# A decoder layer on one core: another issue order, causal bias matmuls of 128 and 64 columns, and shorter constant set-up

## The reference

```python
x = _layernorm(x + attn(x))            # q,k,v with bias; causal softmax over 1024 keys; output projection with bias
x = _layernorm(x + xattn(x, ctx))      # 64 context keys per batch, masked by the mask of batch 0
x = _layernorm(x + ffn(x))             # gate and up to 1024, silu(gate) * up, down to 256
# ffn: ternary weights from mean |w|, activations rounded to 8 bits by each row's maximum
```

## Time and profile before

| | us |
|---|---|
| median of 3 runs (lowest, highest) | 862.05 (861.85, 863.84) |
| profiled execution | 861.85 |
| its span | 860.1 |
| PE busy (share of the span) | 804.4 (94%) |
| DVE busy | 673.9 (78%) |
| ACT busy | 578.8 (67%) |
| POOL busy | 389.6 (45%) |

### The profile page before, as it was taken

One profiled execution on the slowest core, in us unless ns is written; L12 is line 12 of the kernel. 1 busy time (PEld: TensorE's weight loads), 2 busy tenths in 40 slices (PEclk: granted clock), 3 DMA queues, 4 the chain that ended last, 5 costly groups with the idle time before them and its releaser, 6 DMA issues.

```text
span 860.1 us, 21760 instructions
## 1 busy us (share of the span) xinstructions
PE 804.4 (94%) x8207; PEld 388.0 (45%) x8235; DVE 673.9 (78%) x1179; ACT 578.8 (67%) x759; POOL 389.6 (45%) x629
## 2 busy tenths in 40 slices
PE   7888999999999999999999999999999999999875
PEld 5433334344553434534464344633545443445533
DVE  5899898668977798768998589874898858836598
ACT  2377865468865698555875669666696569864486
POOL 6724465446443346542535544472534503442335
PEclk9999999999999999999999999999999999999899
DMA  7713224301223212201221111220131000010001
GB/s 227 203 48 91 49 52 106 94 2 34 48 57 94 63 38 55 72 1 30 72 64 38 38 50 46 63 69 14 39 94 32 26 2 2 2 50 2 2 2 50
DMA packets 47814, 45.50 MB, mean 53 GB/s; under 512 B 9698, under 2 KB 43874, under 8 KB 47714
## 3 DMA queue, kind: packets, MB, share of 16 engines
q1 hardware_dynamic: 43698, 39.12, 17.4%
q0 software_dynamic: 1536, 3.15, 1.6%
q10 hardware_dynamic: 2480, 1.84, 0.8%
HBM read 14.55 MB, written 4.19 MB: 22 GB/s over the span
## 4 chain that ended last, share of the span: by engine, by line
PE 73%; DVE 12%; ACT 8%; issue 3%; DMA 1%; POOL 1%; SPq 1%; ACTq 0%; POOLq 0%; DVEq 0%
PE ps L995 14%; PE ps L1010 14%; PE ps L808 10%; PE ps L970 7%; PE ps L823 5%; DVE shift L1324 5%; PE ps L942 3%; PE ps L869 3%; PE ps L954 3%; ACT probs L1113 3%; PE ps L899 2%; PE ps L911 2%; PE ps L797 2%; PE ps L894 2%; PE ps L880 2%
## 5 line engine op out<-in xcount | busy, mean ns | idle before, releaser
L1113 ACT ACTIVATE probs<-ps 128x1024 f32<-128x1024 f32 (+3 forms) x384 | 296.1, 810 | 121.2 <-PE ps L995 119.0
L1324 DVE TENSOR_REDUCE shift<-ps 128x2 f32<-128x1024 f32 (+2 forms) x224 | 248.5, 1143 | 49.5 <-PE ps L970 28.5
L995 PE MATMUL ps<-q_stack,k_stack 64*128 64x512 bf16 (+3 forms) x1536 | 174.3, 325 | 10.9 <-ACT probs L1113 3.2
L1010 PE MATMUL ps<-probs,v_aug 128*32 128x512 f32 (+3 forms) x1536 | 155.7, 495 | 0.1
L697 POOL TENSOR_SCALAR_AFFINE_SELECT probs<-probs 128x512 f32<-128x512 f32 x128 | 80.6, 638 | 154.5 <-ACT probs L1113 153.7
L970 PE MATMUL ps<-k_stack,q_stack 64*128 64x512 bf16 (+3 forms) x768 | 112.2, 326 | 10.8 <-ACT probs L1113 3.8
L995 PEld LDWEIGHTS ps<-q_stack,k_stack 64*128 64x128 bf16 x1536 | 54.8, 94 | 122.4 <-ACT probs L1113 44.9
L1324 DVE TENSOR_REDUCE shift_h<-ps 128x4 bf16<-128x512 f32 (+2 forms) x96 | 96.8, 1043 | 13.9 <-PE ps L976 13.3
L970 PEld LDWEIGHTS ps<-k_stack,q_stack 64*128 64x128 bf16 x768 | 39.8, 93 | 98.8 <-ACT probs L1113 38.6
L1010 PEld LDWEIGHTS ps<-probs,v_aug 128*32 128x32 f32 x1536 | 34.9, 108 | 42.2 <-issue 31.4
L1237 DVE TENSOR_REDUCE shift<-ps 128x8 bf16<-128x512 f32 x64 | 40.1, 683 | 14.9 <-PE ps L880 14.8
(11 more groups left out here) (188 smaller groups left out, 1344.6 us busy)
## 6 DMA issues: line engine op xcount, KB each, us to landing
q_stack<-part_sb SPq DMA_DIRECT2D x168, 64.0 KB, 2.0
k_stack<-part_sb SPq DMA_DIRECT2D x144, 64.0 KB, 2.1
xT<-in_x_cols SPq DMA_DIRECT2D x8, 512.0 KB, 4.0
xt<-in_x SPq DMA_DIRECT2D x8, 512.0 KB, 3.8
out_x<-xt SPq DMA_DIRECT2D x7, 512.0 KB, 2.8
k_stack<-part_sb POOLq DMA_DIRECT2D x48, 64.0 KB, 2.3
q_stack<-shiftT SPq DMA_DIRECT2D x128, 1.0 KB
q_stack<-part_sb ACTq DMA_DIRECT2D x24, 64.0 KB, 2.5
```

The lines of the kernel that those rows point to most:

```text
L995: mm = pe.matmul(ps[:, u.banks[i], 0:BANK - off], k_stack[rows, part, h, kb * P:(kb + 1) * P], q_stack[rows, part, c, h, off:BANK], start= ...
L1010: mm = pe.matmul(ps[DV * i:DV * (i + 1), SUM_BANK, off:BANK], v_aug[:, kb, at:at + DV], probs_of(b, n)[:, i, :], start=first, stop=last)
L1113: act.activation(probs_of(b, n)[:, 2 * p:2 * p + 2, :], pair(u)[:, :, 0:BANK - off], ACT.Exp).then_inc(probs_ready, 1)
L1324: dve.tensor_reduce(to[:, :, pairs[0]:pairs[-1] + 1, qb % TH], pair(u)[:, :, 0:len(pairs) * w].rearrange("p j (h w) -> p j h w", w=w), AX. ...
```

## The change

Four things change. First, the whole string `ORDER` is another one; the number of units of each kind is the same. Second, the causal bias of a group is added by two matmuls of 128 columns (the rows of the first 64 queries) and two of 64 columns (the first 64 keys for the other queries), where it was four of 64 columns; the number of matmuls and of weight loads is the same. Third, `pick_h` has 192 columns for 256, and POOL builds it and `causal` with 4 selections for 12; a `drain` on POOL behind `make_masks` is gone. Fourth, `stir` runs 15 transposes for 25.

```diff
 ORDER = (
-    "ffwr6sfffr0sgr6sr1r0r6sr2m01m45m23r6ggm45m01m23m45r6ffffm01m23gr4m01m56m23a01a45am01a23w6a45m01fffaa23a45am2"
+    "r6sr5sr6sr5r6sgr5m01gm23m45r6m01ggm45m01r6fm23m01m23wfm01m45r3fm01a45w6r3m01a45fffam23m01a45w6a23afm45fa01oa"
...
-        pick_h, causal = sb("pick_h", [P, 2 * P], BF16), sb("causal", [P, P], BF16)
+        pick_h, causal = sb("pick_h", [P, P + HALF], BF16), sb("causal", [P, P], BF16)
...
             for rows in four:
-                made(pool.affine_select(out=pick_h[rows], in_=pick_h[rows], compare_op=ALU.not_equal, fill=1.0, base=0,
-                                        pattern=[[-1, 2 * P]], channel_multiplier=1))
...
+                made(pool.affine_select(out=pick_h[rows], in_=pick_h[rows], compare_op=ALU.not_equal, fill=1.0, base=HALF,
+                                        pattern=[[-1, P + HALF]], channel_multiplier=1))
                 made(pool.affine_select(out=causal[rows], in_=causal[rows], compare_op=ALU.is_ge, fill=NEG, base=0,
-                                        pattern=[[0, 2], [-1, HALF]], channel_multiplier=1))
...
+                                        pattern=[[-1, P]], channel_multiplier=1))
...
                         make_masks()
-                        pool.drain()
...
-                        stir(u, 25)
+                        stir(u, 15)
...
                     if diag:
-                        for part in range(2):
-                            at, keys = slice(part * P, (part + 1) * P), slice(part * HALF, (part + 1) * HALF)
-                            for s, rows in enumerate(four):
-                                mm = pe.matmul(ps[:, u.banks[s], end - P + part * HALF:end - HALF + part * HALF], pick_h[rows, at],
-                                               causal[rows, keys], start=False, stop=part == 1)
+                        for s, rows in enumerate(four):
+                            pe.matmul(ps[:, u.banks[s], end - P:end], pick_h[rows, HALF:P + HALF], causal[rows, :],
+                                      start=False, stop=False)
+                        for s, rows in enumerate(four):
+                            mm = pe.matmul(ps[:, u.banks[s], end - HALF:end], pick_h[rows, 0:P], causal[rows, 0:HALF],
+                                           start=False, stop=True)
```

More of the change, by code:

```diff
@@ L77 @@
[L77 to L79 removed]
+    "r6sr5sr6sr5r6sgr5m01gm23m45r6m01ggm45m01r6fm23m01m23wfm01m45r3fm01a45w6r3m01a45fffam23m01a45w6a23afm45fa01oa"
+    "23afm01a45m23a45aa01m45m23w6cm01wfa45om23saa45ooa01m23or6m45m01axa23fwfm45a23saa01a23m45r6ao23om45wom01a23m4"
+    "5oa01m23a45xow6a01m23a45m01oga23m45o01om23wa45a01oa23a45m01oaa23m01a45gm23m01am45oom23a01oa45m01aa23m45soa01"
@@ new lines @@
+    "am45r6m01ooa23m45a01o23m45sa01om23a45m01a23a45m01oa23m01a45ga23m01a45m23oam01wa45oa23aa01oa45rm23am01a45a23a"
+    "m45a23m01a45gam23om01m45m23r6m01oom23oa45m01ra23o45am01a23a45oaa23m45a01m23goom01awa45oa23aa01m45r6rm01m23a4"
+    "5aa01om45m23a01o01oaa23m45a01em23eaa01m45oa23m01ooogm45a23o01m45a23p01om23m45bm01p6p5a01a23a45opm01m23r6m01p"
+    "a45a23om45rp01m23m45p6m01m23p5pp6p1p0a23bgaop6gm45a01pr3p6p5a01p2p6aa34a01op6m01p24arm01r6m01ra23p45p02p45r6"
+    "p45a01p23m01aa45op23p01a45om23p01om45a23m01p6m23oa01m45p6o01a23a45oa01goa23pm45rm01r6a23m45a01ppaoa23pa45pap"
@@ new lines @@
+    "rom01m23r6a01a45oaa01m23a45p01m45aom23p6m01m45p3p2om01oop6m45gp3o01p2p6p5p3p2a01gpa34m56apr2xppgp1p0a34a56op"
+    "m12aa34a56pppar0p45a23p6p1oa45apa23a01m45ppr6pam01p23p5p6a23a01m45ooop6aa23a01po45aoa23oopa01ppm23p45p6m01p2"
+    "3p6p3papp01otoa45a23m01p6xo45m01ea23p6a23pa01a45oa23om01a45a23pa01m45oam23p45m01a23m45p6m01m23p5pp6p1p0a23op"
+    "6aa23pm45ba01am23a01p6p1p0a23oap6a23m45a01op6oom01p24om01r6m01p23p04rp23r6a23p01p45m01a23p45rp01o23om45p01om"
+    "23a01m45p6m01m23a45p6a01a23gopa45pa01am23m45a23m01m45a23apoa01a23aa45poa01pm23paa45m01r6m23oom01p45m23a01m45"
@@ new lines @@
+    "p6m23op1gm45ap0m23orp6m45p1p0m23p6o45p1p0a23p6m45a01paoa23a45ppapp6p1a23a45ar0pa23pm45oom01prpa23om45aor6o01"
+    "p23p5p6a01m23a45m01aa23a45goapa23m01a45pppop23m45p6p1ap0a45oopoa23pppp01p6ro45m23oa45m01p23p6m45p3ppa01a45p6"
+    "p3p2p01oca45m01p6m23p5pa01a23gm45oa01pm23r6m01a45aa23ora45am01p23om45a01m23p6a01m23p5pp6tp3aa01p2a45ap6a01m4"
+    "5opea23m01oooa45p6p3a01p2a45p6o01a23p6gm45p02m45r6m45p01p24rbp01op01m23p45m01a23p45a01p23om45p01m23om45a01p6"
+    "m01a23am45p6a01m23a45poapa01a23m45r6am01a23m45a23gom01paa23oa45pm23opaopm01m45rr6a23ga01m45p23m01om45m23p6p1"
@@ L80 @@
+    "p01a45p6op01a23aa45p6p1a23papa45a01p6p3p2p45ooa01op6p5ta01o23poa45a01a23a45poa01a23ooaa01p45a23oaa01a45p6aa0"
+    "1ea23p5pp6p3p2oaoboop6o01pu01p6p5p3p2u1p6v23p04uuv6vu23p01p24p01vu6p01up23v45u6u1p23up45v6u5vu3p01v6v5u3p2vu"
+    "04v6v3p2u04v6pv02u45pv02u45u01pv23u01v23v45u6ppuv01v6pup01p6vuvvp5p3up2p1up0p6p5up3p2pu23pvppp1p6pu5u3u6vpu2"
+    "pvpu5u1p34p6p5v01uuuppuppp56p3p2v1u0p3u2v0puv6v5v3puppv2p01up6vp45vuvvv3v2u01p6p5vu34vvvpv01u6u5uv01pv6v5vut"
+    "tvt"
 )
```

60 lines of the change are left out of this document (15 added, 45 removed).

## The result

The changed kernel takes 889.55 us (median of 4 runs, 888.61 to 890.96) for 861.95 us before: a ratio of 1.032, 95% interval 1.0295 to 1.0344. The sign was right, the size was not: +8 us was forecast, +27.6 us is measured, and 889.55 lies above the range's upper end of 877.

What follows compares the result with a forecast made beforehand. PE was taken to bound the middle (129 to 731 us), DVE the opening and the last 46 us. 861.85 - 3.5 (start) + 5.3 (bias) + 6.0 (order) = 869.65, median 869.9 us; 8-in-10 range 860.5 to 877.

Steps and rivals of the forecast that it cites:

- start: Opening: first DVE subtraction 5.0 us earlier, 0.5 us from the shorter stir, casts cost 2.0; minus 3.5 us in sum.
- bias: Causal bias groups on PE: 27.5 ns more each, paid by the 192 groups outside batch 0; plus 5.3 us.
- new order: PE's middle stretch: more bank reuses too close to cover ACT's or DVE's emptying; plus 6 us, ends -2 and +14.
- drain on POOL: Removed drain behind the masks: put at no cost because POOL is busy under half of the span; 0 us.
- idle 17.2 us: PE's idle time from 129 to 731 us in the kernel before, where PE was said to set the pace.
- the part for the casts: Opening: casts moved from DVE's free time into the stretch where DVE is the bound; plus 2.0 us within start.
- 76 short places in both orders: Opening: bank reuses too close to cover the emptying, 31.0 us before and 35.6 now; cited against rival 2.
- Rival 4: Causal bias costs per instruction, by the skill page's count: 15.8 us for 5.3, 880.4 us in sum; chance 0.03.
- scaled by what the trace before shows, 17.2 us idle for 30.1 us short: Middle: PE idle time taken proportional to bank-reuse shortfall, so 44.6 us short gives 25.5 us idle, plus 8.3 us.
- near 23: PE's idle time in the middle 600 us of the changed profile: near 23 us for 17.2.
- The last 46 us: End, where DVE is the bound: its units keep nearly the same sequence; 0 us, upper end 1 us.
- Rival 5: The new order in PE's stretch is worse than taken: +14 us, 877.9 us in sum; chance 0.10.

Runs made afterwards that it cites:

- e6: Kernel before, only the first 26 units of ORDER changed: context mask cast and five weight loads behind the first splits; 858.93 us, ratio 0.9954.
- e2: Changed kernel with before's order, 25 transposes and the drain, so only the bias and its set-up differ from before; 867.1 us, ratio 1.006.
- e1: Kernel before with only the new string ORDER; 879.1 us, ratio 1.0206.
- e3: Changed kernel with the drain on POOL put back behind make_masks; 885.08 us, ratio 1.0271.
- e8: Kernel before without the drain on POOL behind make_masks; 864.9 us, ratio 1.0041.
- e13: Kernel before with a 128-row, 2-column matmul in front of 143 maxima, making 286 more shape changes; 887.14 us, ratio 1.0263.
- e14: Control of e13: kernel before with the same 143 extra matmuls, but of 64 rows, so no shape change is added; 863.99 us, ratio 1.0014.
- e5: e1 with its middle order loosened until the distances between users of a bank fell as short as in before's order; 887.87 us, ratio 1.0303.
- e7: e6 with its order loosened over its whole length by the same bank-distance rule as e5; 868.23 us, ratio 1.0084.
- e9: e1 with its order reworked by playing the four engines' rows against each other, 157 units moved; 880.85 us, ratio 1.0215.
- e11: Kernel before with exponentials and maxima doing only a quarter of their columns (first 12 steps' exponentials kept full); 841.92 us, ratio 0.9748.
- e12: e1 with the same quarter-length exponentials and maxima as e11; 854.64 us, ratio 0.9906.
- e10: e6 with its order reworked by the same four-engine bookkeeping as e9, 104 units moved; 863.24 us, ratio 1.0007.
- e15: e6 with its order reworked by bookkeeping that also prices changes of array shape, 110 units moved; 866.02 us, ratio 1.0035.

## Why the prediction was wrong, point by point

| term | forecast us | measured us | from |
|---|---|---|---|
| start | -3.5 | -2.4; by the ratio -4.0 (-6.3 to -1.7) | e6 |
| bias | +5.3 | +6.0 | e2 |
| new order | +6 (-2 to +14) | about +20 to +22 | e1 less the start: 18.0 + 2.4 to 4.0 |
| drain on POOL | 0 | +4.5 (0.4 to 8), in before +3.5 (1.8 to 5.2) | after less e3; e8 |
| sum | +7.8 | +28 | +27.6 measured |

**What bounds the kernel.** Right as far as it goes: PE sets the middle, and the bias is paid there nearly in full. But "idle 17.2 us" was taken for all that PE loses there. Counted from start to start, the same order loses some 30 us to waits in that part and 54 us more to changes of shape (e6), most of which the page writes down as busy.

**Start.** The early first subtraction and the size are right (e6); the part for the casts isn't shown. In the whole change the gain is given back before 129 us: counted from start to start, PE has done its first 105 us of work 0.9 us later in e1 than in before, though its first maximum came about 5 us earlier. The prediction had read "76 short places in both orders" in the opening, "by 31.0 us before and 35.6 now", and left the order's cost there out of the sum.

**Bias.** Right. 27.5 ns a group was read from a pair of 512 columns; the group takes 0.09 for 0.06 us in the trace, and the time is 6.0 for 5.3 us. Rival 4 (bias per instruction, 15.8 us) is excluded by e2's interval (3 to 7.3 us).

**The new order.** This step failed, "scaled by what the trace before shows, 17.2 us idle for 30.1 us short". Its idle time came out as said (6.3 us more in e1 than in e6; that the whole kernel has 24.3 for "near 23" owes 3.53 us to the drain), but two things were missing. First, the step began with "the work is the same and only the waits can change". It is not the same: 67 changes of shape more, 6.7 us by the traces, 5.0 by e13 and e14. Second, the measure doesn't carry: with the shortfall of before, e5 is the slowest order of all, and e7 and e9 show the same for other reworkings. By place, of the 20 to 22 us some 6 lie in the opening and 13 in the middle. By kind, 5 to 7 are changes of shape (their number times their price; no run takes them away), about 5 (0 to 9) are waits for long exponentials and maxima (e11, e12), and some 8 to 12 are open. They are still there when the takers are short. The waits of PE that grew from e11 to e12 are many and small; the ones for POOL, e11 first, in two executions that are only 6.0 of the 12.7 us apart:

```profile
PE ps L789 <- POOL region L740: 2.1, 3, 1.3
PE ps L789 <- POOL k_stack L740: 1.5, 2, 0.9
```

```profile
PE ps L789 <- POOL region L740: 2.9, 2, 1.6
PE ps L1010 <- POOL probs L697: 1.9, 1, 1.9
PE ps L789 <- POOL k_stack L740: 2.2, 2, 1.4
```

(us in total, times, longest.) No experiment here separates them.

**No cost.** The drain was put at 0 "since POOL is busy under half of the span". A share of the span says nothing of one place: 2 us of draining were moved from 38.6 us, where nobody waited, to 161.7 us, in front of `q_mask`, where PE stood 3.53 us and then ran at a clock of 0.50 (3.3 us in the trace, what is left of 4.5 lies within the noise). What had covered the drain, and what happens where that cover is gone, wasn't asked. The last 46 us: 0 was right. Of 46 us PE is busy 29.39 in e1 for 30.04, DVE 38.18 for 38.48.

**Rivals.** All of them moved one of the terms that were seen. None had a price for the term that was set to nothing (the drain) or for one that no idle row shows (the change of shape). Rival 5, +14 for the order, pointed the right way and was still 6 to 8 us short.

## What to carry to other kernels

When units are only reordered, count what lies between them as well as the waits: here every step between matmuls of different array shapes costs 0.09 to 0.12 us, in both directions, and stands in the profile as busy time, so compare busy time of equal matmuls and distances from start to start. The drain on POOL took as long as the DMAs issued since the last one were many, so removing it moved its cost to the next one; ask who waits there, and what the wait does to the clock. And a rule for "looser" orders must first rank orders whose time is known: of five reworkings made here by such rules (e5, e7, e9, e10, e15) none was faster than what it was made from, while the one edit that was read straight off the timeline, e6, was.

## What the runs showed that was not expected

- A drain on POOL behind 24 of its DMAs takes 2.0 us, behind 48 it takes 3.99 us, and with none issued since the last one mostly 0.034 to 0.046 us; this is so long after the last of them was issued (at 119 us, the drain at 161.7).
- A change of array shape costs 0.094 to 0.117 us, the most when it leaves 128x32; 143 extra matmuls of 2 columns in the shape at hand cost together 1.2 us (interval -1.3 to 3.7).
- Neighbouring reductions on DVE overlap in their records: 1.22 us long, 1.13 us from start to start; exponentials of 1024 columns 1.02 and 0.92.
